# A graph layer on one core: queries' rows stored apart from the values, and the first edge pair's gathers and feature parts made in the first block

## The chip, the cores and the metric

The kernel runs on one core of one Trainium2 chip. The metric is the device time of one execution in microseconds (us). A core has five instruction streams that work side by side: TensorE (PE, matrix products), VectorE (DVE), ScalarE (ACT), GpSimd (POOL) and SyncE (SP, which here only issues DMAs). POOL and ACT issue DMAs too.

## The reference

One layer on N = 1250 nodes and E = 20000 edges with 512 features and 8 heads of 64: graph attention over the edges, a linear attention beside it, and a small quantised feed-forward behind both. Edges are sorted by destination. The part that the change touches is the graph attention:

```python
x_cat = jnp.concatenate([node_feat[src], node_feat[dst], edge_feat], axis=-1)
r = x_cat @ Wr.T + br
q = (node_feat @ Wq.T + bq).reshape(n, H, D)
k = (r @ Wk.T + bk).reshape(e, H, D)
v = (r @ Wv.T + bv).reshape(e, H, D)
a = jnp.einsum('ehd,ehd->eh', q[dst], k) * scaler
amax = jax.ops.segment_max(a, dst, num_segments=n)
ae = jnp.exp(a - amax[dst])
asum = jax.ops.segment_sum(ae, dst, num_segments=n)
attn = ae / asum[dst]
m = v * attn[..., None]
out = jax.ops.segment_sum(m, dst, num_segments=n).reshape(n, H * D)
```

## The kernel before

The program has two blocks with a barrier of all engines between them: `prologue` (the first block) and `edges_and_ending`. Every product in fp32 precision is made as three products of a high and a low part (`_hi`, `_lo`: ACT copies to the high part, DVE subtracts it for the low part).

**First block.** Weights are multiplied together first (`fold(part)`: 96 products each; part 0 for sources, 1 for destinations, 2 for edge features), so that a node's and an edge's share of keys and values is one product each. Then `source(t)` makes the rows of `kv_table` for the ten node tiles t of 128 nodes. Behind `fold(1)` comes the **destination stage**: for each t, PE makes the queries `destination_q`, the own key share `destination_k` and the own value share `destination_v`; DVE adds biases (`add_q`, `own_scores`, `add_v2`), writes the queries' rows with their own scores into `q_out` (two buffers) and the values into `v2_out` (two buffers); SP stores them to `q_table` and `v2_table` (`store_nodes(t)`). In the profile, names ending in a digit lose it: `v_out` and `v_table` are `v2_out` and `v2_table`.

Between these, PE makes `cuts(k)` for 40 quads k of four edge tiles: products of `onehot` (made by DVE in `one_hots(k)`) with `is_end16`. ACT copies each result to `cut_out` (two buffers), and POOL stores it to `cut_rows`. The chain of one quad is DVE one-hots, PE `cuts(k)`, ACT copy k, POOL store k. PE's `cuts(k)` waits for copy k - 2, and ACT's copy k waits until store k - 2 has landed. ACT also runs `sign_group` (12 row comparisons each) in between, and at k = 0, 6, 12 and 18 issues a **clear**: a DMA that fills one 2.6 MB `merge` table with its start values.

The program order on PE is, per t: `cuts(4t-2)`, `cuts(4t-1)`, k(t), `cuts(4t)`, v(t), `cuts(4t+1)`, q(t+2). On DVE, per t: `add_q(t+1)`, `own_scores(t)`, for some t a `rank_group`, `one_hots(4t+4)`, `(4t+5)`, `add_v2(t)`, `one_hots(4t+6)`, `(4t+7)`. The waits that guard the two buffers are:

```python
def add_q(t):      # and add_v2(t) alike
    if t >= 2:
        dve.wait_ge(stored[u], 16 * (NT // 2) + 32 * (t // 2))
```

`stored[u]` counts the stores of queries and of values together, so each of them waits until both stores of t - 2 have landed. `fold(2)` ends the block on PE; `evict(2)` on ACT and DVE splits its eight banks, and the barrier follows.

**Second block.** It runs over 79 pairs p of edge tiles. SP loads the pair's features (`efT`, pair 0's in `first_ef` already in the first block) and rows of indices; POOL gathers `kv` by source and `qc` by destination and `old` from the merge tables by indirect DMA, and stores `new`. PE makes `keys` (psK, 12 products a tile) and `values` (psV) of two tiles, then `sort_scores(p)`, which needs DVE's scores of the pair (`add_k`, `times_q`, `sum_scores`, `split_scores`, `rank_one_hots`). At the block's start, in the kernel before, come POOL's `fetch_kv(0)` and `fetch_q(0)` and, for pair 0, ACT's `high_part(0)` and DVE's `low_part(0)`. Behind the pairs comes the ending (linear attention, output, feed-forward).

Of the kernel before, what the change touches and what calls it, by code (L numbers as in the profile page):

```python
# [12 lines left out]
F32 = mybir.dt.float32  # L13
# [3 lines left out]
ALU = mybir.AluOpType  # L17
# [42 lines left out]
def layer(nc, x, src_col, dst_col, dst_row, ef, WqT, bq, Wr, br, WkT, bk, WvT, bv, WoT, bo, gamma, beta,  # L60
# [10 lines left out]
    with top:  # L71
# [20 lines left out]
        with ExitStack() as early:  # L92
# [12 lines left out]
            prologue(nc, ef, ef_in[0], first_ef, x, WqT, bq, Wr, br, WkT, bk, WvT, bv, src_col, dst_col, dst_row, q_table, kv_table, v2_table, merge,  # L105
# [7 lines left out]
            edges_and_ending(nc, ef, ef_in, first_ef, q_table, kv_table, merge, ident, M_hi, M_lo, dst_rows, end_rows, cut_rows,  # L113
# [5 lines left out]
def prologue(nc, ef, first_ef_in, first_ef, x, WqT, bq, Wr, br, WkT, bk, WvT, bv, src_col, dst_col, dst_row, q_table, kv_table, v2_table, merge,  # L119
# [3 lines left out]
    with ExitStack() as ctx:  # L123
# [12 lines left out]
        Wq_hi = sb("Wq_hi", [P, C, D], F32R)  # L136
        Wq_lo = sb("Wq_lo", [P, C, D], F32R)
# [11 lines left out]
        kv_out = sb("kv_out", [P, 2, 2 * D])  # L149
# [20 lines left out]
        hi_split, lo_split, br_hi_ready, br_lo_ready = sem("hi_split"), sem("lo_split"), sem("br_hi_ready"), sem("br_lo_ready")  # L170
# [5 lines left out]
        q_added, kd_added, own_step, v2_added = sem("q_added"), sem("kd_added"), sem("own_step"), sem("v2_added")  # L176
        stored = [sem(f"nodes_stored{i}") for i in range(2)]
        tables_out, cleared = sem("tables_out"), sem("cleared")
# [35 lines left out]
        def _(sp):  # L214
# [52 lines left out]
            for i in range(2):  # L267
                sp.wait_ge(stored[i], 48 * (NT // 2))

        @block.gpsimd  # L270
        def _(pool):
# [29 lines left out]
            for k, (lo, n) in enumerate(quads):  # L301
                if k == 2:
                    load_block(LATE + 2)
                if k == 6:
# [7 lines left out]
                           ends_out[0:ET - P, 1, :]).then_inc(tables_out, 16)  # L312
            pool.wait_ge(tables_out, 16 * 3)
# [1877 lines left out]
```

## Time and profile before

| | |
|---|---|
| runs of the kernel before | 1622.1 us median of 3 (1619.85 to 1623.33) |
| the profiled execution's own time | 1626.55 us |
| its span in the trace | 1624.8 us |
| PE busy | 1551.1 us, 95% of the span |
| DVE, ACT, POOL busy | 77%, 65%, 43% |
| DMA mean | 185 GB/s |

All positions in the trace are us from the span's start. An engine's row gives when it began and how long it took; in square brackets stands how long the engine had stood idle before it, and what the profile takes to have released it. Where a wait has several semaphores the profile names the one that came last, and where the engine named had long been done it was another. The granted clock of PE (PEclk) is 1.00 at 2.4 GHz and 0.50 at 1.2 GHz.

### The profile page before, as it was taken

What the parts mean: (1) busy time and instruction counts of PE and PEld (TensorE: products, weight loads), DVE (VectorE), ACT (ScalarE), POOL (GpSimd) and SP (SyncE); (2) the same over time, 40 slices, a digit from 0 to 9 for tenths busy, and PEclk for the clock granted to TensorE, in tenths of its full rate; (3) what the DMA queues carried; (4) which work ended last, traced back from release to release, by engine and by line L of the source; (5) the groups of instructions that cost most, each with busy time, mean ns of one, the idle gap of its engine ahead of it and who ended that gap; (6) DMA issues with size and microseconds to landing.
All of it is one profiled execution on the core that took longest, in us unless ns stands there. A gap on an engine that the chain in (4) does not pass through costs nothing. (4 is left out here: it accounts for less than half of the span.)

```text
span 1624.8 us, 27304 instructions
## 1 busy us (share of the span) xinstructions
PE 1551.1 (95%) x7334; PEld 1202.1 (74%) x7334; DVE 1256.3 (77%) x3141; ACT 1054.6 (65%) x3706; POOL 694.3 (43%) x722
## 2 busy tenths in 40 slices
PE   7999898999999999999999999999999999899996
PEld 6786676777777777777777777777777777777673
DVE  5866664887788778788788778878877878678878
ACT  3785122677777777777777777777777777567245
POOL 1001123556555555555555565555555565211001
PEclk9999999999999999999999999999999999999997
DMA  6575414666666666666676666666666666175001
GB/s 194 180 247 181 174 67 137 200 215 202 210 208 207 224 211 216 211 199 199 201 239 218 198 218 204 211 206 212 220 208 209 202 201 198 45 236 192 27 14 51
DMA packets 135446, 300.31 MB, mean 185 GB/s; under 512 B 34863, under 2 KB 56502, under 8 KB 135296
## 3 DMA queue, kind: packets, MB, share of 16 engines
q0 software_dynamic: 63600, 180.17, 33.6%
q1 hardware_dynamic: 66512, 107.59, 22.2%
q10 hardware_dynamic: 5184, 10.81, 1.8%
q8 instruction: 62, 1.02, 0.3%
q14 instruction: 88, 0.72, 0.1%
HBM read 271.40 MB, written 66.58 MB: 208 GB/s over the span
## 5 line engine op out<-in xcount | busy, mean ns | idle before, releaser
L1110 ACT ACTIVATE wv<-vv,expd 128x64 f32<-128x64 f32 x1248 | 314.6, 334 | 2.7
L1122 ACT ACTIVATE old<-old,expd 128x64 f32<-128x64 f32 x1232 | 302.1, 334 | 0.0
L1032 POOL DMA_INDIRECT merge<-new,put_id x157 | 162.8, 1037 | 269.2 <-DVE new L1453 236.9
L1882 PE MATMUL psK<-M_hi,efT_hi 128*128 128x512 f32 x628 | 254.3, 405 | 2.8 <-ACT efT_hi L1080 2.8
L1882 PE MATMUL psV<-M_hi,efT_hi 128*128 128x512 f32 x628 | 256.1, 408 | 0.0
L1883 PE MATMUL psK<-M_lo,efT_hi 128*128 128x512 f32 x628 | 250.0, 398 | 0.0
L1883 PE MATMUL psV<-M_lo,efT_hi 128*128 128x512 f32 x628 | 249.5, 397 | 0.0
L1003 POOL DMA_INDIRECT old<-merge,dst_id x157 | 157.8, 1005 | 142.6 <-DMA merge<-new,put_id 116.9
L1096 ACT ACTIVATE expd<-diff 128x32 f32<-128x32 f32 (+1 forms) x79 | 18.1, 229 | 289.3 <-DVE diff L1432 289.3
L1003 POOL DMA_INDIRECT kv<-kv_table,src_id x157 | 162.3, 1034 | 66.1 <-issue 47.8
L1003 POOL DMA_INDIRECT qc<-q_table,dst_id x157 | 155.0, 987 | 54.6 <-issue 46.6
L1886 PE MATMUL psK<-M_hi,efT_lo 128*128 128x512 f32 x628 | 172.3, 396 | 0.0
L1886 PE MATMUL psV<-M_hi,efT_lo 128*128 128x512 f32 x628 | 171.9, 395 | 0.0
L1882 PEld LDWEIGHTS psK<-M_hi,efT_hi 128*128 128x128 f32 x628 | 119.0, 190 | 28.2 <-ACT efT_hi L1080 3.2
L1886 PEld LDWEIGHTS psK<-M_hi,efT_lo 128*128 128x128 f32 x628 | 118.2, 188 | 28.8
L1886 PEld LDWEIGHTS psV<-M_hi,efT_lo 128*128 128x128 f32 x628 | 118.0, 188 | 28.8
L1883 PEld LDWEIGHTS psK<-M_lo,efT_hi 128*128 128x128 f32 x628 | 119.3, 190 | 25.8
L1883 PEld LDWEIGHTS psV<-M_lo,efT_hi 128*128 128x128 f32 x628 | 119.1, 190 | 25.6
L1882 PEld LDWEIGHTS psV<-M_hi,efT_hi 128*128 128x128 f32 x628 | 118.8, 189 | 25.1
L1384 DVE TENSOR_TENSOR runs_lo<-psT,runs_hi 128x16 fp32r<-128x16 f32 (+1 forms) x79 | 13.7, 174 | 144.0 <-ACT runs_hi L1087 144.0
L1344 DVE TENSOR_TENSOR kk<-psK,kv 128x512 f32<-128x512 f32 x157 | 107.0, 681 | 13.5 <-DMA kv<-kv_table,src_id 10.0
L1353 DVE TENSOR_TENSOR kq<-kk,qc 128x520 f32<-128x520 f32 x157 | 110.0, 701 | 6.6 <-DMA qc<-q_table,dst_id 1.2
(323 smaller groups left out, 3334.7 us busy)
## 6 DMA issues: line engine op xcount, KB each, us to landing
first_ef<-in_ef_turned_dram SPq DMA_DIRECT2D x39, 512.0 KB, 5.0
efT<-in_ef_turned_dram SPq DMA_DIRECT2D x39, 512.0 KB
merge<-empty ACTq DMA_DIRECT2D x4, 2640.0 KB, 10.0
rows<-merge SPq DMA_DIRECT2D x40, 256.0 KB, 3.7
row_block<-dst_rows POOLq DMA_DIRECT2D x13, 768.0 KB, 6.1
dst_line<-dst_rows SPq DMA_DIRECT2D x78, 128.0 KB, 2.7
end_line<-end_rows SPq DMA_DIRECT2D x78, 128.0 KB, 4.3
kv_table<-kv_out SPq DMA_DIRECT2D x10, 512.0 KB, 3.2
```

The costliest lines, as they stand in the source:

```text
L1003: pool.indirect_dma_start(out=out, out_offset=None, in_=table[:, :], in_offset=bass.IndirectOffsetOnAxis(ap=ids[:, t:t + 1], axis=0)).then ...
L1032: pool.indirect_dma_start(out=merge[2 * (p % 2) + u][:, :], out_offset=bass.IndirectOffsetOnAxis(ap=put_id[:, t:t + 1], axis=0), in_=new[p ...
L1096: act.activation(expd[p % 2][:, 0:n, :, :], diff[p % 2][:, 0:n, :, :], ACT.Exp, scale=SCALE).then_inc(exp_ready, 1)
L1110: act.activation(wv[:, u, h * DH:(h + 1) * DH], vv[p % 2][:, u, h * DH:(h + 1) * DH], ACT.Copy, scale=expd[p % 2][:, u, 0, h:h + 1]).then_ ...
L1122: act.activation(rows, rows, ACT.Copy, scale=expd[p % 2][:, u, 1, h:h + 1]).then_inc(old_scaled, 1)
L1344: dve.tensor_tensor(kk[:, u, :, 0:DH], psK[u][:, :].rearrange("p (h d) -> p h d", h=H), kv[p % 2][:, u, 0:D].rearrange("p (h d) -> p h d", ...
L1353: dve.tensor_tensor(kq[:, u, :, :].rearrange("p h e -> p (h e)"), kk[:, u, :, :].rearrange("p h e -> p (h e)"), qc[p % 2][:, u, :], ALU.mu ...
L1384: dve.tensor_tensor(runs_lo[:, 0:n, :], turned_s[:, 0:n, :], runs_hi[:, 0:n, :].bitcast(F32), ALU.subtract).then_inc(runs_low, 1)
L1882: pe.matmul(out[:, :], efT_hi[b][:, u, c, :], Me_hi[:, c, col:col + D], start=c == 0, stop=False)
L1883: pe.matmul(out[:, :], efT_hi[b][:, u, c, :], Me_lo[:, c, col:col + D], start=False, stop=False)
L1886: last = pe.matmul(out[:, :], efT_lo[b][:, u, c, :], Me_hi[:, c, col:col + D], start=False, stop=c == C - 1)
```

## The change

1. **Queries' rows apart.** `store_nodes(t)` issues the queries' store first, as soon as `own_scores(t)` is done, and counts it on a semaphore of its own, `q_stored`; then it waits for the values and issues their store on `stored`. `add_q(t)` waits for the queries' store of t - 2 alone, `add_v2(t)` for the values' store alone. To free semaphores, `kd_added` is folded into `own_step` (three steps a tile), and two others into `br_split`.
2. **The first gathers.** The buffers of pair 0 (`efT_hi0`, `efT_lo0`, `kv0`, `qc0`) are placed over tensors of the first block that are dead by then (`kv_out`, `Wq_hi`, `br_hi` and `br_lo`, which are moved in memory for it). POOL issues the two gathers of `kv0` and the two of `qc0` at the end of its first-block work, behind waits that all stores of the tables have landed.
3. **The first features' parts.** ACT's `high_part(0)` and DVE's `low_part(0)` stand in the first block, between the last split of `fold(2)`'s inputs and `evict(2)`.

```diff
+            kv_in = [top.enter_context(nc.semaphore(f"kv_in{i}")) for i in range(2)]
+            q_in = [top.enter_context(nc.semaphore(f"q_in{i}")) for i in range(2)]
+            hi_ready, lo_ready = (top.enter_context(nc.semaphore(n)) for n in ("efT_hi_ready", "efT_lo_ready"))
+            with ExitStack() as place:
+                def head(name, shape, dt=F32):
+                    return place.enter_context(nc.sbuf_tensor(name, shape, dt))
+
+                efT1 = head("efT1", [P, 2, C, P])
+                efT_hi1, efT_lo1, efT_hi0, efT_lo0 = (
+                    head(n, [P, 2, C, P], F32R) for n in ("efT_hi1", "efT_lo1", "efT_hi0", "efT_lo0"))
+                kv = [head(f"kv{b}", [P, 2, 2 * D]) for b in range(2)]
+                qc = [head(f"qc{b}", [P, 2, QROW]) for b in range(2)]
+            efT, efT_hi, efT_lo = [first_ef, efT1], [efT_hi0, efT_hi1], [efT_lo0, efT_lo1]
...
         raw = sb("raw", [P, SLOTS - 2, D])
+        kv_out = sb("kv_out", [P, 2, 2 * D])
+        Wq_hi = sb("Wq_hi", [P, C, D], F32R)
+        Wq_lo = sb("Wq_lo", [P, C, D], F32R)
+        br_hi = sb("br_hi", [P, C, P], F32R)
+        br_lo = sb("br_lo", [P, C, P], F32R)
+        bias = sb("bias", [P, 2, D])
         W_hi = sb("W_hi", [P, 2, C, D], F32R)
         W_lo = sb("W_lo", [P, 2, C, D], F32R)
...
-        br_hi = sb("br_hi", [P, C, P], F32R)
-        br_lo = sb("br_lo", [P, C, P], F32R)
-        bias = sb("bias", [P, 2, D])
...
-        kv_out = sb("kv_out", [P, 2, 2 * D])
...
             def store_nodes(t):
+                sp.wait_ge(own_step, 3 * t + 3)
+                sp.dma_start(q_table[t * P:(t + 1) * P, :],
+                             q_out[:, t % 2, :, :].rearrange("p h e -> p (h e)")).then_inc(q_stored[t % 2], 16)
                 sp.wait_ge(v2_added, t + 1)
                 sp.dma_start(v2_table[t * P:(t + 1) * P, :], v2_out[:, t % 2, :]).then_inc(stored[t % 2], 16)
-                sp.wait_ge(own_step, 2 * t + 2)
-                sp.dma_start(q_table[t * P:(t + 1) * P, :],
-                             q_out[:, t % 2, :, :].rearrange("p h e -> p (h e)")).then_inc(stored[t % 2], 16)
...
             for i in range(2):
-                sp.wait_ge(stored[i], 48 * (NT // 2))
+                sp.wait_ge(stored[i], 32 * (NT // 2))
+                sp.wait_ge(q_stored[i], 16 * (NT // 2))
...
                            ends_out[0:ET - P, 1, :]).then_inc(tables_out, 16)
+            pool.wait_ge(ids_in, 32)
+            pool.wait_ge(nodes_done, destination_at("v", NT - 1))
+            for i in range(2):
+                pool.wait_ge(stored[i], 32 * (NT // 2))
+                pool.wait_ge(q_stored[i], 16 * (NT // 2))
+            for u in range(2):
+                pool.indirect_dma_start(out=kv0[:, u, :], out_offset=None, in_=kv_table[:, :],
+                                        in_offset=bass.IndirectOffsetOnAxis(ap=src_id[:, u:u + 1], axis=0)).then_inc(kv0_in, 16)
+            for u in range(2):
+                pool.indirect_dma_start(out=qc0[:, u, :], out_offset=None, in_=q_table[:, :],
+                                        in_offset=bass.IndirectOffsetOnAxis(ap=dst_id[:, u:u + 1], axis=0)).then_inc(q0_in, 16)
...
                 if t >= 2:
-                    pe.wait_ge(kd_added, t - 1)
+                    pe.wait_ge(own_step, 3 * t - 5)
...
             split_wr(2 * C + 3)
+            for i in range(2):
+                act.wait_ge(stored[i], 32 * (NT // 2))
+            act.wait_ge(first_ef_in, 16)
+            act.activation(efT_hi0[:, :, :, :], first_ef[:, :, :, :], ACT.Copy).then_inc(hi_ready, 1)
             evict(2)
...
                 u = t % 2
                 dve.wait_ge(nodes_done, destination_at("q", t))
                 if t >= 2:
-                    dve.wait_ge(stored[u], 16 * (NT // 2) + 32 * (t // 2))
+                    dve.wait_ge(q_stored[u], 16 * (t // 2))
                 dve.tensor_tensor(q_out[:, u, :, 0:DH], banks[3 * u][:, :].rearrange("p (h d) -> p h d", h=H),
...
                 dve.wait_ge(nodes_done, destination_at("k", t))
                 if t >= 1:
-                    dve.wait_ge(own_step, 2 * t - 1)
-                dve.tensor_tensor(kd[:, :], banks[3 * u + 1][:, :], bias[:, 0, :], ALU.add).then_inc(kd_added, 1)
-                dve.wait_ge(kd_added, t + 1)
+                    dve.wait_ge(own_step, 3 * t - 1)
+                dve.tensor_tensor(kd[:, :], banks[3 * u + 1][:, :], bias[:, 0, :], ALU.add).then_inc(own_step, 1)
+                dve.wait_ge(own_step, 3 * t + 1)
                 dve.wait_ge(q_added, t + 1)
-                if t >= 1:
-                    dve.wait_ge(own_step, 2 * t)
                 dve.tensor_tensor(own[:, :].rearrange("p (h d) -> p h d", h=H), kd[:, :].rearrange("p (h d) -> p h d", h=H),
                                   q_out[:, u, :, 0:DH], ALU.mult).then_inc(own_step, 1)
-                dve.wait_ge(own_step, 2 * t + 1)
+                dve.wait_ge(own_step, 3 * t + 2)
                 dve.tensor_reduce(q_out[:, u, :, DH], own[:, :].rearrange("p (h d) -> p h d", h=H),
                                   AX.X, ALU.add).then_inc(own_step, 1)
...
                 if t >= 2:
-                    dve.wait_ge(stored[u], 16 * (NT // 2) + 32 * (t // 2))
+                    dve.wait_ge(stored[u], 16 * (NT // 2) + 16 * (t // 2))
                 dve.tensor_tensor(v2_out[:, u, :], banks[3 * u + 2][:, :], bias[:, 1, :], ALU.add).then_inc(v2_added, 1)
...
             split_wr(2 * C + 2)
             split_wr(2 * C + 3)
+            dve.wait_ge(hi_ready, 1)
+            dve.tensor_tensor(efT_lo0[:, :, :, :], first_ef[:, :, :, :], efT_hi0[:, :, :, :].bitcast(F32),
+                              ALU.subtract).then_inc(lo_ready, 1)
             evict(2)
...
-            efT = [first_ef, loop("efT1", [P, 2, C, P])]
-            efT_hi, efT_lo = [None, None], [None, None]
-            for b in (1, 0):
-                efT_hi[b], efT_lo[b] = (loop(f"{n}{b}", [P, 2, C, P], F32R) for n in ("efT_hi", "efT_lo"))
-            kv = loop_two("kv", [P, 2, 2 * D])
-            qc = loop_two("qc", [P, 2, QROW])
+            loop("place_of_head", [P, 5 * 2 * C * P + 2 * 2 * 2 * D + 2 * 2 * QROW])
...
-            fetch_kv(0)
-            fetch_q(0)
             for p in range(PAIRS + 2):
                 if p + 1 < PAIRS:
...
-            high_part(0)
             for p in range(PAIRS):
...
             dve.wait_ge(ones_placed, 1)
-            low_part(0)
             for p in range(PAIRS):
```

How the instructions stand, at three places. First SP, in the destination stage, before: the rows of two tiles t (`v_table`, `q_table` are the stores, in square brackets the semaphores that they wait for).

```order
35 L264 DMA first_ef<-in_ef_turned_dram 128x1024 [waits lo_split]
36 L234 DMA v_table<-v_out 128x512 [waits v2_added]
37 L236 DMA q_table<-q_out 128x520 [waits own_step]
38 L234 DMA v_table<-v_out 128x512 [waits v2_added]
39 L236 DMA q_table<-q_out 128x520 [waits own_step]
```

And SP at the same place after the change.

```order
35 L278 DMA first_ef<-in_ef_turned_dram 128x1024 [waits lo_split]
36 L248 DMA q_table<-q_out 128x520 [waits own_step]
37 L251 DMA v_table<-v_out 128x512 [waits v2_added]
38 L248 DMA q_table<-q_out 128x520 [waits own_step]
39 L251 DMA v_table<-v_out 128x512 [waits v2_added]
```

In each tile the queries' store moved ahead of the values' store.

Second POOL, at the boundary of the blocks (the two branches are the end of the first block and the start of the second), before.

```order
25 L310 DMA end_rows<-ends_out 128x128 [waits cut_copied]
26 L311 DMA end_rows<-ends_out 29x128
27 L123 UNCONDITIONAL_BRANCH [waits cut_stored0,cut_stored1,cleared,tables_out]
28 L1000 UNCONDITIONAL_BRANCH [waits barrier_Pool_Activation_PE_DVE_SP_gather]
29 L1003 DMA kv<-kv_table,src_id 128x1024 x2
30 L1003 DMA qc<-q_table,dst_id 128x520 x4
31 L1003 DMA kv<-kv_table,src_id 128x1024 x2
```

POOL at the same place after the change.

```order
25 L325 DMA end_rows<-ends_out 128x128 [waits cut_copied]
26 L326 DMA end_rows<-ends_out 29x128
27 L334 DMA kv<-kv_table,src_id 128x1024 [waits queries_stored0,nodes_stored1,nodes_stored0,queries_stored1,nodes_done,ids_in]
28 L334 DMA kv<-kv_table,src_id 128x1024
29 L337 DMA qc<-q_table,dst_id 128x520 x2
30 L136 UNCONDITIONAL_BRANCH [waits cut_stored0,cut_stored1,cleared,tables_out]
31 L1026 UNCONDITIONAL_BRANCH [waits barrier_Pool_Activation_PE_DVE_SP_gather]
32 L1029 DMA qc<-q_table,dst_id 128x520 x2
33 L1029 DMA kv<-kv_table,src_id 128x1024 x2
```

The four gathers of pair 0 moved ahead of the branch; behind it stand pair 1's.

Third ACT, at the same boundary, before.

```order
123 L461 ACTIVATE wr_hi<-raw 128x512 [waits raw_in0,rounds]
124 L461 ACTIVATE wr_hi<-raw 128x512 [waits raw_in1,rounds]
125 L476 ACTIVATE M_hi<-bank 128x512 [waits folded] x8
126 L123 UNCONDITIONAL_BRANCH
127 L1073 UNCONDITIONAL_BRANCH [waits barrier_Pool_Activation_PE_DVE_SP_release]
128 L1080 ACTIVATE efT_hi<-first_ef 128x1024 [waits ef_in0]
129 L1080 ACTIVATE efT_hi<-efT 128x1024 [waits ef_in1]
```

ACT at the same place after the change.

```order
124 L487 ACTIVATE wr_hi<-raw 128x512 [waits raw_in1,rounds]
125 L575 ACTIVATE efT_hi<-first_ef 128x1024 [waits ef_in0,nodes_stored1,nodes_stored0]
126 L502 ACTIVATE M_hi<-bank 128x512 [waits folded] x8
127 L136 UNCONDITIONAL_BRANCH
128 L1097 UNCONDITIONAL_BRANCH [waits barrier_Pool_Activation_PE_DVE_SP_release]
129 L1104 ACTIVATE efT_hi<-efT 128x1024 [waits ef_in1]
```

The high part of `first_ef` moved ahead of the eight evictions and the branch; DVE's low part moved alike.

## Rows read from the trace of the kernel before

**Rows 1.** Busy time by stretch, in the pairs: PE, PEld, DVE, ACT, POOL, PEclk, DMA share, GB/s

```profile
300.00:700.00 400.00, 394.04 (x1866) 307.87 (x1865) 324.79 (x733) 292.14 (x1071) 224.72 (x223) 1.00 0.65 209
```

**Rows 2.** Waits, 140 to 300 us: us in total, times, longest

```profile
PE bank L395 <- DVE onehot L666: 8.3, 3, 5.1
```

**Rows 3.** Timeline of PE, destination stage: start, us, line, operation

```profile
141.99 0.38 PE L395 MATMUL bank<-onehot,is_end 128*1 128x128 bf16 x4
...
145.29 0.38 PE L395 MATMUL bank<-onehot,is_end 128*1 128x128 bf16 x4
...
151.62 0.59 PE L395 MATMUL bank<-onehot,is_end 128*1 128x128 bf16 x4 [2.64 <-DVE onehot L666]
...
157.56 0.43 PE L395 MATMUL bank<-onehot,is_end 128*1 128x128 bf16 x4
...
182.95 0.59 PE L395 MATMUL bank<-onehot,is_end 128*1 128x128 bf16 x4 [5.07 <-DVE onehot L666]
...
188.69 0.38 PE L395 MATMUL bank<-onehot,is_end 128*1 128x128 bf16 x4
```

**Rows 4.** Busy time by stretch around two stops of PE, columns as Rows 1

```profile
148.00:163.00 15.00, 12.36 (x51) 8.65 (x50) 7.08 (x36) 6.11 (x23) 2.67 (x6) 0.77 0.63 220
...
260.00:268.00 8.00, 5.23 (x17) 3.83 (x16) 3.15 (x5) 2.10 (x3) 4.13 (x4) 0.79 0.50 141
```

**Rows 5.** Timeline of DVE, destination stage

```profile
176.11 0.69 DVE L674 TENSOR_TENSOR q_out<-bank,bq_all 128x512 f32<-128x512 f32 x1 [8.01 <-DMA q_table<-q_out]
```

**Rows 6.** Timeline of SP's DMA issues, destination stage

```profile
166.93 1.26 SPq L236 DMA_DIRECT2D q_table<-q_out  x1
```

**Rows 7.** DMA, 152.2 to 156 us: packets, MB, share by queue; landing us

```profile
q10 hardware_dynamic: 693, 1.46, 102.8%
...
cut_rows<-cut_out POOLq DMA_DIRECT2D x2, 2.0 KB, 6.5
```

**Rows 8.** Timeline of ACT, destination stage

```profile
145.79 0.59 ACT L539 ACTIVATE cut_out<-bank 1x512 f32<-1x512 f32 x1 [4.04 <-DMA cut_rows<-cut_out]
...
150.91 1.05 ACT L539 ACTIVATE cut_out<-bank 1x512 f32<-1x512 f32 x2
...
176.97 1.07 ACT L539 ACTIVATE cut_out<-bank 1x512 f32<-1x512 f32 x2 [4.41 <-DMA cut_rows<-cut_out]
```

**Rows 9.** DMA, 140 to 143 us

```profile
DMA packets 396, 1.02 MB, mean 340 GB/s; under 512 B 68, under 2 KB 68, under 8 KB 396
...
cut_rows<-cut_out POOLq DMA_DIRECT2D x2, 2.0 KB, 4.0
```

**Rows 10.** Timeline of POOL at the block boundary

```profile
243.99 0.54 POOL L311 DMA_DIRECT2D end_rows<-ends_out  x1
262.88 1.04 POOL L1003 DMA_INDIRECT kv<-kv_table,src_id  x1 [18.35 <-POOLq L123]
```

**Rows 11.** Timeline of PE, block boundary and pairs 0 and 1

```profile
263.26 0.62 PE L1882 MATMUL psK<-M_hi,efT_hi 128*128 128x512 f32 x1 [2.77 <-ACT efT_hi L1080]
...
273.31 0.40 PE L1882 MATMUL psV<-M_hi,efT_hi 128*128 128x512 f32 x1
...
275.18 1.10 PE L1886 MATMUL psV<-M_hi,efT_lo 128*128 128x512 f32 x4
280.43 0.23 PE L1909 MATMUL psO<-to_rank,score_hi 128*8 128x128 f32 x1 [4.15 <-DVE to_rank L1323]
...
280.74 0.73 PE L1882 MATMUL psK<-M_hi,efT_hi 128*128 128x512 f32 x1
...
284.14 1.09 PE L1886 MATMUL psK<-M_hi,efT_lo 128*128 128x512 f32 x4
```

**Rows 12.** Timeline of DVE, pair 0

```profile
274.26 0.69 DVE L1344 TENSOR_TENSOR kk<-psK,kv 128x512 f32<-128x512 f32 x1 [9.73 <-DMA kv<-kv_table,src_id]
...
279.96 0.42 DVE L1323 TENSOR_TENSOR to_rank<-iota_row,rank 128x256 fp32r<-128x256 f32 x1
```

**Rows 13.** DMA issues, 262 to 285 us

```profile
first_ef<-in_ef_turned_dram SPq DMA_DIRECT2D x1, 512.0 KB, 12.5
```

More of the change, by code:

```diff
@@ L104, in layer @@
             ef_in = [top.enter_context(nc.semaphore(f"ef_in{i}")) for i in range(2)]
[L105 removed]
+            kv_in = [top.enter_context(nc.semaphore(f"kv_in{i}")) for i in range(2)]
[10 more added lines that the diff above has]
+            efT, efT_hi, efT_lo = [first_ef, efT1], [efT_hi0, efT_hi1], [efT_lo0, efT_lo1]
+            prologue(nc, ef, ef_in[0], first_ef, efT_hi0, efT_lo0, hi_ready, lo_ready, kv[0], kv_in[0], qc[0], q_in[0], x, WqT, bq, Wr, br, WkT, bk, WvT, bv, src_col, dst_col, dst_row, q_table, kv_table, v2_table, merge,
                      dst_rows, end_rows, cut_rows, ident, xT_hi, xT_lo, M_hi, M_lo, src_id, dst_id, put_id, dst_f, rank,
@@ L112, in layer @@
             wq_lo = early.enter_context(nc.sbuf_tensor("wq_lo", [P, C, D], F32R, side="right"))
-            edges_and_ending(nc, ef, ef_in, first_ef, q_table, kv_table, merge, ident, M_hi, M_lo, dst_rows, end_rows, cut_rows,
+            edges_and_ending(nc, ef, ef_in, efT, efT_hi, efT_lo, hi_ready, lo_ready, kv, kv_in, qc, q_in, q_table, kv_table, merge, ident, M_hi, M_lo, dst_rows, end_rows, cut_rows,
                              src_id, dst_id, put_id, dst_f, rank, iota_row, iota_col, w_qkv, w_raw, wq_hi, wq_lo,
@@ L116, in layer, with prologue @@
                              res, wp, wp_lo, gT, later, out, stored)
-def prologue(nc, ef, first_ef_in, first_ef, x, WqT, bq, Wr, br, WkT, bk, WvT, bv, src_col, dst_col, dst_row, q_table, kv_table, v2_table, merge,
+def prologue(nc, ef, first_ef_in, first_ef, efT_hi0, efT_lo0, hi_ready, lo_ready, kv0, kv0_in, qc0, q0_in, x, WqT, bq, Wr, br, WkT, bk, WvT, bv, src_col, dst_col, dst_row, q_table, kv_table, v2_table, merge,
              dst_rows, end_rows, cut_rows, ident, xT_hi, xT_lo, M_hi, M_lo, src_id, dst_id, put_id, dst_f, rank,
@@ L169, in prologue @@
         bias_in, ids_in, rows_cast, consts = sem("bias_in"), sem("ids_in"), sem("rows_cast"), sem("consts")
-        hi_split, lo_split, br_hi_ready, br_lo_ready = sem("hi_split"), sem("lo_split"), sem("br_hi_ready"), sem("br_lo_ready")
+        hi_split, lo_split, br_split = sem("hi_split"), sem("lo_split"), sem("br_split")
         rounds, folded, m_hi, m_lo = sem("rounds"), sem("folded"), sem("m_hi"), sem("m_lo")
@@ L175, in prologue @@
         nodes_done, ks_copied, vs_copied = sem("nodes_done"), sem("ks_copied"), sem("vs_copied")
-        q_added, kd_added, own_step, v2_added = sem("q_added"), sem("kd_added"), sem("own_step"), sem("v2_added")
+        q_added, own_step, v2_added = sem("q_added"), sem("own_step"), sem("v2_added")
         stored = [sem(f"nodes_stored{i}") for i in range(2)]
+        q_stored = [sem(f"queries_stored{i}") for i in range(2)]
         tables_out, cleared = sem("tables_out"), sem("cleared")
@@ L403, in between_edge_part @@
                 if i == 1:
-                    pe.wait_ge(kd_added, NT)
+                    pe.wait_ge(own_step, 3 * NT - 2)
                 if i == 3:
@@ L418, in _ @@
             fold(0)
-            pe.wait_ge(br_lo_ready, 1)
+            pe.wait_ge(br_split, 2)
             for side in range(2):
@@ L497, in _ @@
                     act.wait_ge(bias_in, 16)
-                    act.activation(br_hi[:, :, :], bc(br_col[:, :], P), ACT.Copy).then_inc(br_hi_ready, 1)
+                    act.activation(br_hi[:, :, :], bc(br_col[:, :], P), ACT.Copy).then_inc(br_split, 1)
             for t in range(4):
@@ L602, in _ @@
                 if rc == 0:
-                    dve.wait_ge(br_hi_ready, 1)
+                    dve.wait_ge(br_split, 1)
                     dve.tensor_tensor(br_lo[:, :, :], bc(br_col[:, :], P), br_hi[:, :, :].bitcast(F32),
-                                      ALU.subtract).then_inc(br_lo_ready, 1)
+                                      ALU.subtract).then_inc(br_split, 1)
             for t in range(4):
@@ L774, in ending_tensors, with edges_and_ending @@
             y, yT_lo, fst, fmv, fsd, xs, hs, xn, xr, xq, xqT, hid, hq, hqT, ys, fy)
-def edges_and_ending(nc, ef, ef_in, first_ef, q_table, kv_table, merge, ident, Me_hi, Me_lo, dst_rows, end_rows, cut_rows,
+def edges_and_ending(nc, ef, ef_in, efT, efT_hi, efT_lo, hi_ready, lo_ready, kv, kv_in, qc, q_in, q_table, kv_table, merge, ident, Me_hi, Me_lo, dst_rows, end_rows, cut_rows,
                      src_id, dst_id, put_id, dst_f, rank, iota_row, iota_col, w_qkv, w_raw, wq_hi, wq_lo, xT_hi, xT_lo,
@@ L847, in edges_and_ending @@
         row_in, cut_in = ([sem(f"{n}{b}") for b in range(2)] for n in ("row_in", "cut_in"))
-        kv_in, q_in, old_in, put = ([sem(f"{n}{b}") for b in range(2)] for n in ("kv_in", "q_in", "old_in", "put"))
+        old_in, put = ([sem(f"{n}{b}") for b in range(2)] for n in ("old_in", "put"))
         def landed(p):
             return 16 * sum(tiles_of(k) for k in range(p % 2, p + 1, 2))
-        hi_ready, lo_ready, ke_done, ve_done = sem("efT_hi_ready"), sem("efT_lo_ready"), sem("k_edges"), sem("v_edges")
+        ke_done, ve_done = sem("k_edges"), sem("v_edges")
         ones_placed, onehots = sem("ones_placed"), sem("onehots")
```

2 lines of the change are left out of this document (removed).

## The prediction

> **What bounds the kernel now.** First the busy time by stretch in the pairs: PE is busy 394.04 of 400 us at full clock, the next engine, DVE, 324.79 [rows 1]. From pair 2 on PE therefore sets the pace, and whatever makes PE start there earlier moves the whole rest of the run. So I looked for PE's idle time before that, in the list of waits and then in PE's timeline from 140 to 290 us. In the destination stage PE stands 8.3 us in three waits, the longest 5.1 [rows 2]; the two large ones are 2.64 us at 151.62 and 5.07 us at 182.95 [rows 3]. At the block boundary it stands 2.77 us, and 4.15 us at 280.43 before pair 0's scores are sorted [rows 11]. The reader should see a second loss behind each: the granted clock, 0.77 in the stretch around the first and 0.79 around the boundary [rows 4], that is, a piece at 1.2 GHz between pieces at 2.4. Its price can be read: from one `cuts` to the next with a product between is 3.30 us undisturbed (141.99 to 145.29), but 5.94 us behind the first wait (151.62 to 157.56) and 5.74 behind the second (182.95 to 188.69) [rows 3]. So the clock costs 2.64 and 2.44 us on top of the idle time.
>
> **Who causes them.** The second wait: DVE stood 8.01 us until 176.11 at `add_q(4)`, for the queries' store of t = 2 [rows 5], which SP issued at 166.93 [rows 6], so 9.2 us from issue to landing. PE then waits for one-hots that stand behind it on DVE. The first wait is named DVE's too, but those one-hots (quad 7) were made long before; what `cuts(7)` also needs is ACT's copy of quad 5, and that stands in the row of two copies from 150.91 [rows 8], behind a `sign_group` which itself began after copy 4. Copy 4 was held 4.04 us, to 145.79, by the landing of the store of quad 2 [rows 8].
>
> **Why a store lands so late.** From 152.2 to 156 us, behind a clear's issue, only the ACT queue's packets ran, 693 of them at 102.8% of the engines, and cut rows issued there took 6.5 us to land [rows 7]. A store that is issued into a clear waits for it; one that is issued ahead of it doesn't. The Trainium skill (DMA: Bandwidth & Descriptors, section Queues, rings and completion order) says that each DMA engine serves the queues with work in turn, a packet at a time. The trace disagrees here: with stores of two other queues outstanding it shows a single queue's 693 packets. By that rule small stores would pass a clear, and the third case below would have no ground.
>
> **Part 1, queries' rows apart.** No instruction is added but one wait; the number of stores stays. The queries' store leaves right after `own_scores(t)`, thus ahead of the one-hots and, at some t, a rank group and the values' sum; and `add_q(t+1)` no longer waits for the values' store. Stage by stage: PE's k(2) would end near 156.8, so the store of t = 2 leaves near 159, ahead of the clear at k = 12, instead of at 166.93 behind its issue. Then it lands well before DVE wants the buffer for `add_q(4)`. DVE has no other long wait in the tile, so quad 16's one-hots are ready about 3.5 us before PE asks. The second wait goes entirely: 5.07 + 2.44 = 7.5 us. What is late next there is ACT's copy 14, which `cuts(16)` needs: it starts at 176.97 [rows 8] against PE's wish at 182.95 - 5.07 = 177.88 [rows 3], 0.3 us in time if a copy takes some 0.6.
>
> The first wait is hardly touched, since it belongs to ACT. Only one of its causes moves: the store of quad 2 landed 4.0 us after its issue, in a stretch with 1.02 MB at 340 GB/s [rows 9]. The queries' store of t = 0, 260 KB, leaves that stretch (it would be issued some 5 us earlier): 0.26 MB / 340 GB/s = 0.8 us. Copy 4, the sign group and copy 5 follow by as much. Bounds: nothing (0) if the landing doesn't depend on it, and 2.64 + 2.64 = 5.3 us if copy 5 comes in time. I take 0.8, idle time only, because 1.8 us of idle remains and every stop of that order in this trace had the low clock behind it. The third wait, the remaining 0.6 us of the 8.3, I leave. Part 1: 7.5 + 0.8 = 8.3 us.
>
> **Part 2, the first gathers.** In the kernel before, POOL is free at 243.99 + 0.54 = 244.5 and then idle for 18.35 us up to its first gather at 262.88 [rows 10]. DVE's first sum waits 9.73 us for it until 274.26, and `to_rank` of pair 0 is only done at 280.4 [rows 12]; PE ended pair 0 at 276.28 (275.18 + 1.10) and waits 4.15 us for it [rows 11]. After the change the four gathers are issued from about 244.5, at some 1.3 us each (until 250), while PE still makes `fold(2)`, whose DMA traffic is nearly nil; their landing needs at most the 12.5 us of the slowest transfer in the crowded start [rows 13], so by 262.5 in the worst case, and DVE wants them at about 266. DVE then follows PE: `to_rank` about 272.5, before PE's end of pair 0 at 275.4. The 4.15 us go. With them goes the low clock behind: the eight products from 280.74 to 284.14 took 3.40 us, the same eight at full clock 275.18 - 273.31 = 1.87 [rows 11], thus 1.53 more. Part 2: 5.7 us. Next in line is pair 1's data; the gathers and loads of pairs 1 and 2 start as before at the block's start with 1.6 MB less ahead of them.
>
> **Part 3, the first parts.** ACT's copy (1.06 us) and DVE's subtraction (1.23) go into a hole of about 5 us on both engines between the last split and the evictions; they are covered by PE's `fold(2)`. If the cover were gone they would cost their 2.3 us. PE's start in the second block no longer follows ACT's copy. Its idle time of 2.77 us [rows 11] holds the eviction and the barrier as well, which stay; I count 0.9 of the copy's 1.06 as gained, since PE must load its first weights. Bounds 0 and 1.1. I leave the low clock behind the boundary as it is: 1.9 us of idle remains. If it stayed at full clock, 1.5 us more would be gained.
>
> **The sum.** 8.3 + 5.7 + 0.9 = 14.9 us off the profiled execution's own 1626.55 (span 1624.8 and 1.75 around it) gives 1611.6. The median of the runs, 1622.1, is 4.4 below that execution; the same 14.9 off it gives **1607.2 us**. Nothing later gives it back: PE paces pairs 2 to 78 [rows 1].
>
> **The ways it could go.**
> - *As above*, 1607.2, chance 0.50; its own range 1604.5 to 1609.5 (the clock at the boundary and the unknown of each part).
> - *ACT's chain comes free too.* Copy 5 is in time, since the store of quad 2 lands as fast as an undisturbed one. For it: 2.5 us earlier would be nearly the 2.64 needed. Against it: the row block of 768 KB and the clears stay. Another 1.84 + 2.64 = 4.5 us: 1602.7. Chance 0.18.
> - *The cut chain takes the place of the queries' wait.* Copy 14 has only 0.3 us of slack and its stores run beside a clear, 6.5 us to land [rows 7]. If PE then stops 2 us at `cuts(16)` and the clock falls as before: 2.0 + 2.4 back, 1611.6. Chance 0.17.
> - *The second block starts as before*: gathers are early, but pair 1's features or gathers stop PE instead, since PE now asks 5 us sooner. Only part 1 stays: 1622.1 - 8.3 = 1613.8. Against it: less is outstanding. Chance 0.09.
> - *Slower.* One mechanism: with all requests of pairs 1 and 2 made at once, `efT` of pair 1 lands late, PE stops before pair 1 and falls to the low clock. It needs 12.5 us at worst [rows 13] from 263.4, thus 276 and a copy of 1.06, against 275.7: 1.4 us of stop. To decide it would have to land over 15 us later, 28 us after issue; at 32 us the time is 1626. Chance 0.02.
> - The rest, 0.04, lies about no change (a store or gather held by something that no row shows).
>
> A measurement of this kernel tells 0.2% (3.2 us) from no change. All cases but the last two are beyond it: faster 0.93, same 0.05, slower 0.02. The range 1601.0 to 1612.5 reaches over the first three cases, 0.85, and leaves out the tails of each.
>
> **What would show it.** In the profile after: no wait of `add_q` for a store above 1 us; PE without idle time near 178 to 183 and at full clock there; PE's wait near 151 still there, 1 to 2.6 us, and the clock low behind it; POOL's gathers of `kv` from 244 to 250 less the shift; PE's first psK product 1.7 to 2 us behind the last of `fold(2)`; no wait before `sort_scores(0)`; pairs of the same length as before. Wrong would be: a new wait at `cuts(16)` or near k = 18 released by ACT's copies or stores of cut rows; a wait of ACT for `efT` that PE follows; or the gathers of pair 0 issued only at the barrier.

## The result and the profile after

The changed kernel takes 1605.17 us (median of 5 runs, 1602.33 to 1606.27), the kernel before 1622.1 us (1619.85 to 1623.33, 5 runs). The ratio is 0.9893, with a 95% interval of 0.988 to 0.9907: 16.9 us or 1.1% faster. The forecast was 1607.2 us, 14.9 less.

The page of the changed kernel, first busy times:

```profile
span 1603.4 us, 27308 instructions
PE 1540.9 (96%) x7334; PEld 1194.8 (75%) x7334; DVE 1257.7 (78%) x3141; ACT 1054.7 (66%) x3706; POOL 688.4 (43%) x722
```

PE's own waits from 100 to 300 us, where [rows 2] had 8.3 us in the destination stage alone:

```profile
PE psK L1904 <- PEq L136: 1.7, 1, 1.7
PE bank L421 <- ACT cut_out L565: 1.1, 2, 0.8
PE bank L421 <- DVE onehot L696: 0.5, 1, 0.5
```

The first of these is the block boundary. What is left at the place of the first stop of [rows 3] stands in PE's timeline, with the product and the `cuts` behind it:

```profile
146.94 0.38 PE L421 MATMUL bank<-onehot,is_end 128*1 128x128 bf16 x4 [0.82 <-ACT cut_out L565]
...
150.21 0.38 PE L421 MATMUL bank<-onehot,is_end 128*1 128x128 bf16 x4
```

From one `cuts` to the next it is now 3.27 us behind the stop, where [rows 3] show 5.94: the clock didn't fall. Over 45 us of the stage it shows as this (windows; busy us and count of PE, PEld, DVE, ACT, POOL, then granted clock, DMA share, GB/s), first before, then after:

```profile
145.00:190.00 45.00, 37.29 (x166) 26.59 (x165) 27.13 (x114) 12.80 (x40) 6.99 (x15) 0.85 0.44 158
```

```profile
145.00:190.00 45.00, 43.91 (x228) 31.73 (x227) 34.14 (x132) 12.43 (x29) 9.92 (x20) 1.00 0.64 237
```

The two windows don't hold quite the same work, but both of the first profile's stops lie in its window. PE's idle time in these 45 us falls from 7.7 to 1.1 us, and the granted clock rises from 0.85 to 1.00: both losses that the prediction read there are gone.

**What each store does now.** SP's and ACT's issues in the stage, and DVE's `add_q(4)` and `add_q(5)`:

```profile
141.39 0.32 SPq L248 DMA_DIRECT2D q_table<-q_out  x1
...
145.66 0.37 ACTq L558 DMA_DIRECT2D merge<-empty  x1
...
152.48 0.32 SPq L248 DMA_DIRECT2D q_table<-q_out  x1
...
159.17 0.69 DVE L704 TENSOR_TENSOR q_out<-bank,bq_all 128x512 f32<-128x512 f32 x1
...
159.20 0.37 ACTq L558 DMA_DIRECT2D merge<-empty  x1
...
162.93 0.32 SPq L248 DMA_DIRECT2D q_table<-q_out  x1
...
170.53 0.69 DVE L704 TENSOR_TENSOR q_out<-bank,bq_all 128x512 f32<-128x512 f32 x1 [0.62 <-DMA q_table<-q_out]
```

The queries' store of t = 2 leaves at 152.48, 6.7 us ahead of the clear at 159.20, and lands in 3.9 us; in [rows 6] it left at 166.93, behind a clear, and took 9.2. `add_q(4)` runs at 159.17 without a wait, against 176.11 in [rows 5]. The next store, t = 3 at 162.93, does fall behind a clear and takes 7.5 us, but DVE comes for its buffer so late that it waits 0.62 us. The landing times come from the DMA view of 152 to 155 us and of 160 to 164:

```profile
q_table<-q_out SPq DMA_DIRECT2D x1, 260.0 KB, 3.9
```

```profile
q_table<-q_out SPq DMA_DIRECT2D x1, 260.0 KB, 7.5
```

DVE's waits for stores of queries fell from 27.0 us in six waits to 0.6 in one.

**The start of the second block.** POOL, then PE:

```profile
230.24 1.04 POOL L334 DMA_INDIRECT kv<-kv_table,src_id  x1 [0.30 <-issue]
...
234.13 0.96 POOL L337 DMA_INDIRECT qc<-q_table,dst_id  x1 [0.30 <-issue]
248.18 0.95 POOL L1029 DMA_INDIRECT qc<-q_table,dst_id  x1 [13.09 <-POOLq L136]
```

```profile
247.58 0.47 PE L1904 MATMUL psK<-M_hi,efT_hi 128*128 128x512 f32 x1 [1.69 <-PEq L136]
258.87 0.22 PE L1931 MATMUL psO<-to_rank,score_hi 128*8 128x128 f32 x1
```

All four gathers are issued before PE is through with the block, the hole before `psK` is 1.69 us instead of 2.77, and the 4.15 us before `sort_scores(0)` of [rows 11] are gone.

**A ledger by stage.** Read from PE's rows: S1 is the time from the last product of `fold(1)` to the first of `fold(2)` (the destination stage), S2 from the last of `fold(2)` to `sort_scores(2)`. `fold(2)` itself is 22.5 us in every profile. From pair 2 on, executions differ by more than the change is worth with nothing changed (the changed kernel took 1041.8 us from `sort_scores(2)` to `sort_scores(75)` in one profile and 1061.5 in another), so parts of the change are compared in these stretches, and whole runs only where they were timed in turn with the kernel before.

| profile | S1 | S2 |
|---|---|---|
| kernel before; the same again | 114.5; 112.7 | 48.4; 47.8 |
| changed kernel; the same again | 102.7; 102.8 | 39.9; 39.9 |
| stores apart only | 103.5 | 48.3 |
| gathers and parts only; the same again | 111.6; 114.4 | 39.9; 39.9 |
| change, gathers back | 103.1 | 47.8 |
| change, parts back | 102.6 | 41.0 |
| change, values' store first | 112.9 | 39.9 |
| change, both waits | 108.5 | 39.9 |
| before, clears late | 109.2 | 49.9 |
| before, signs earlier | 105.7 | 48.5 |
| change, signs earlier | 105.4 | 39.9 |

The change takes 9.9 to 11.8 us out of S1 and 7.9 to 8.5 out of S2, 17.8 to 20.3 together, by which pair of profiles one takes. The two spans first profiled differ by 21.4 us; 2.8 of that lie ahead of S1, where nothing of the change works: both have two stops of about one us near 40 us, and only in the profile before 3.4 us of half clock follow. (One other profile of the fourteen, experiment 2's second, has the same.) The rest of the spans tells the other way: from `sort_scores(2)` to the end the kernel before took 1316.7 and 1315.2 us, the changed kernel 1318.4 and 1338.1. So in the first pair of profiles 1.7 us of the 20.3 don't reach the end. Whether the change causes that or it is the spread of executions is not shown.

### The profile page after: what moved, and what is told of

It reads as the page before. It is cut to its first block and busy times, and to the rows that moved or that the text cites. A ratio compares the mean times of both kernels' runs of the same rounds, so it can differ in the third digit from the quotient of the medians.

```text
span 1603.4 us, 27308 instructions
## 1 busy us (share of the span) xinstructions
PE 1540.9 (96%) x7334; PEld 1194.8 (75%) x7334; DVE 1257.7 (78%) x3141; ACT 1054.7 (66%) x3706; POOL 688.4 (43%) x722
## 5 line engine op out<-in xcount | busy, mean ns | idle before, releaser
L1029 POOL DMA_INDIRECT kv<-kv_table,src_id x155 | 155.3, 1002 | 47.8 <-issue 47.5
L1385 DVE TENSOR_REDUCE score<-kq 128x8 f32<-128x520 f32 x157 | 109.1, 695 | 5.4
```

The source lines that it names most:

```text
L1029: pool.indirect_dma_start(out=out, out_offset=None, in_=table[:, :], in_offset=bass.IndirectOffsetOnAxis(ap=ids[:, t:t + 1], axis=0)).then ...
L1385: dve.tensor_reduce(score[p % 2][:, u, :], kq[:, u, :, :], AX.X, ALU.add).then_inc(score_step, 1)
```

## The experiments

The kernels of the first four experiments (of the second, its first run) ran beside the kernel before, which there took from 1623.2 to 1649.5 us in 34 of its 35 runs and 1679.8 in one. So of them only the ratio and the stretches are used, and all whole-run differences between them are within their intervals.

**1. The stores apart, alone.** The changed kernel with gathers and parts at the start of the second block again:

```diff
-            for u in range(2):
-                pool.indirect_dma_start(out=kv0[:, u, :], out_offset=None, in_=kv_table[:, :],
...
-            act.activation(efT_hi0[:, :, :, :], first_ef[:, :, :, :], ACT.Copy).then_inc(hi_ready, 1)
...
+            fetch_kv(0)
+            fetch_q(0)
...
+            high_part(0)
...
+            low_part(0)
```

> Part 1 alone: queries' stores apart and first, but the first gathers and the first high and low parts back in the second block. Theory A (the ledger of the profile after): PE's two stops in the destination stage go, 1.8 and 5.1 us of idle, and the low clock behind both, 2.6 and 2.4, together 11.9 us: 1610. The gap of 2.8 us at the boundary and the 4.2 us before pair 0's scores are sorted stay, with the low clock behind both. Rival B (as my prediction priced it, ACT's chain hardly touched): 8.3 us, 1613.8. Rival C (the surplus over the forecast comes from the run's start, not from part 1): the stop near 147 us is 1.8 us or more here.

Measured: 1621.47 us, ratio 0.9928 (0.9891 to 0.9964). S1 is 103.5 and S2 48.3: the whole gain of the destination stage and nothing of the boundary's. The first stop was 0.88 us, and S1 is 9.2 to 11.0 us shorter. So theory A holds: the surplus over the forecast is the stage's own (B had 8.3 us in all) and doesn't come from the run's start (C). PE's timeline has both holes of before back:

```profile
248.38 0.51 PE L1890 MATMUL psK<-M_hi,efT_hi 128*128 128x512 f32 x1 [2.77 <-ACT efT_hi L1088]
265.39 0.23 PE L1917 MATMUL psO<-to_rank,score_hi 128*8 128x128 f32 x1 [3.99 <-DVE to_rank L1331]
```

**2. Gathers and parts, alone.** The values' store goes first again, and each sum waits for both stores of t - 2:

```diff
+                sp.wait_ge(v2_added, t + 1)
+                sp.dma_start(v2_table[t * P:(t + 1) * P, :], v2_out[:, t % 2, :]).then_inc(stored[t % 2], 16)
                 sp.wait_ge(own_step, 3 * t + 3)
...
-                sp.wait_ge(v2_added, t + 1)
-                sp.dma_start(v2_table[t * P:(t + 1) * P, :], v2_out[:, t % 2, :]).then_inc(stored[t % 2], 16)
...
                     dve.wait_ge(q_stored[u], 16 * (t // 2))
+                    dve.wait_ge(stored[u], 16 * (NT // 2) + 16 * (t // 2))
...
                     dve.wait_ge(stored[u], 16 * (NT // 2) + 16 * (t // 2))
+                    dve.wait_ge(q_stored[u], 16 * (t // 2))
```

> Parts 2 and 3 alone: values stored first again, and both sums wait again for both stores of t - 2. Theory A: the destination stage shows the two stops of before again (2.6 and 5.1 us, low clock behind both), the boundary looks as after the change: 4.2 + 1.5 for the gathers, 1.1 for the parts, and 1.7 if the clock stays full at the boundary, 6.8 to 8.5 us: 1614 to 1615.3. Rival: if the parts don't add up (one hides the other), this and the run before it together give back clearly more or less than the 16.9 us of the whole.

Measured: 0.9945 (0.9912 to 0.9979). S2 is 39.9, and the second stop is back, 6.64 us:

```profile
177.08 0.58 PE L421 MATMUL bank<-onehot,is_end 128*1 128x128 bf16 x4 [6.64 <-DVE onehot L696]
```

But the first stop was only 0.68 us, with the stores in their old order. That didn't fit the view that the queries' early store shortens it, so the kernel was run once more.

> Parts 2 and 3 alone, once more. In the first run of it PE's first stop was 0.7 us only, although the queries' store of t = 0 was issued as late as before the change. If it is the position of that store that delays the landing of quad 2's store, 2 us or more of stop should be seen in this second look; if the landing is 2 us again, something else in this kernel (addresses, counting apart) does it.

It had 2.22 us there, 6.54 at the second, and 1617.97 us in the one run. So the landing that decides the first stop differs from one execution to the next. ACT's wait before copy 4 was 3.5 to 4.2 us in five profiles with the old order and 2.08 in the first run of these parts; it was 1.5 to 2.3 in all six with the early store and the sign groups in their place.

**3. The gathers back, alone** (`fetch_kv(0)` and `fetch_q(0)` at the second block's start; parts stay early).

> The changed kernel with only the four gathers of pair 0 back at the start of the second block. Theory: DVE's first sum waits for them some 9 us again, PE stands 4 us before the sorting of pair 0 and has the low clock behind it: 5.7 us over the changed kernel, 1610.9. Rival: the parts made early let PE start sooner, so PE waits longer for the same gathers and part 3's gain is lost as well: 5.7 + 1.1, 1612.

Measured: 0.9935 (0.9901 to 0.997), S2 47.8, as much as before. PE's start is early (1.69 us of idle), but it pays that back at the scores:

```profile
266.27 0.28 PE L1922 MATMUL psO<-to_rank,score_hi 128*8 128x128 f32 x1 [6.20 <-DVE to_rank L1337]
```

The gathers' path ends last here, so what PE gains at the boundary lengthens its wait for them, 4.15 to 6.20 us. Early parts are worth nothing without early gathers. In S2 that is 7.9 us over the changed kernel; the theory had 5.7, the rival that loses part 3's gain as well had 6.8 and was right in kind.

**4. The parts back, alone** (`high_part(0)` and `low_part(0)` at the second block's start; gathers stay early).

> The changed kernel with only the high and low part of pair 0 back in the second block. Theory: PE's gap at the boundary is 2.8 instead of 1.7 us, 1.1 us more, and the granted clock falls to 0.5 behind it as before the change, another 1.5 to 1.7: 1607.9. Rival: the clock's fall there is not tied to the gap's length and comes and goes from run to run: 1606.3, and a profile that may show full clock behind 2.8 us of idle.

Measured: 0.9928 (0.9895 to 0.9961), S2 41.0. So early parts are worth 1.1 us beside early gathers, which is the hole's 2.77 less 1.69:

```profile
247.80 0.51 PE L1899 MATMUL psK<-M_hi,efT_hi 128*128 128x512 f32 x1 [2.77 <-ACT efT_hi L1097]
```

The clock stayed at 2.4 GHz behind this hole, as in no other profile with a hole of 2.77 (five had 3.4 to 6.8 us at 1.2 GHz behind it). So the expectation's rival is what this profile shows, and 1.1 us is the price at full clock; where the clock falls it would be more.

**5. The change again**, timed beside the next three.

> The changed kernel once more, on the chip of the three runs beside it, so that they can be compared, and for the low clock behind gaps of 1 to 1.7 us in a second profile: ratio 0.989 to 0.990. If the clock's falls at 41 us and at the block boundary come and go from run to run, this profile may show one of them.

Measured: 1613.91 us where the kernel before had 1625.64, ratio 0.9917 (0.9891 to 0.9942). The clock fell neither at 41 us nor at the boundary.

**6. Is it the order of the stores, or the waits apart?** The changed kernel with the values' store first, the waits still apart (the first half of experiment 2's edit).

> The changed kernel with the values' store ahead of the queries' again, each still counted apart. It tells early issue from split waits. Theory: it is the early issue that counts. The queries' store of t = 0 then stands in the stretch of the row block again, quad 2's store lands 4 us after its issue, PE stops 2.6 us near 147 with the low clock behind it, and the queries' stores of t = 1 and t = 2 lie in the clears again, so that DVE waits for them some 6 to 8 us and PE stops near 178: 1614 to 1617, most of part 1 lost. Rival: the split of the waits counts, and the time stays at 1605 to 1608.

Measured: 0.9953 (0.9927 to 0.9979). S1 is 112.9: nothing of the stage's gain is left. PE's timeline:

```profile
148.39 0.38 PE L421 MATMUL bank<-onehot,is_end 128*1 128x128 bf16 x4 [2.13 <-DVE onehot L696]
...
179.79 0.59 PE L421 MATMUL bank<-onehot,is_end 128*1 128x128 bf16 x4 [6.30 <-DVE onehot L696]
```

and DVE's waits from 140 to 230 us:

```profile
DVE q_out L704 <- DMA q_table<-q_out: 26.8, 7, 7.9
```

**7. The queries' store first, but each sum waits for both stores** (the second half of that edit).

> The changed kernel with the queries' store first, but each sum waiting for both stores of t - 2 again. Theory: add_q(3) then waits for the values' store of t = 1, issued at 147 behind the clear and landing near 155, and add_q(5) for that of t = 3, issued at 168 in the second clear and landing near 174; PE has some 3 us of slack behind DVE there, so it stops less than before the change: 0 to 3 us of idle in all, 1605 to 1610. Rival: the values' store takes the whole place of the queries' store, PE stops 5 us near 178 and the clock falls: 1612.

Measured: 0.9951 (0.9926 to 0.9976), S1 108.5, about half of the gain. The theory's 0 to 3 us of idle time was wrong and the rival right, the values' store takes the queries' place:

```profile
DVE q_out L705 <- DMA v_table<-v_out: 20.3, 6, 6.4
```

```profile
174.26 0.38 PE L421 MATMUL bank<-onehot,is_end 128*1 128x128 bf16 x4 [4.97 <-DVE onehot L696]
```

The first stop is gone in it (no idle time at `cuts(7)`), the second isn't, and the clock falls behind it. Both halves of part 1 are needed: the wait apart is worth nothing as long as the queries' store goes last, and the early store gives only the first stop while the sums wait for the values' too.

**8. The kernel before with the clears of k = 6, 12 and 18 made late**, to see whether the clears make the stores land late:

```diff
-                if k % 6 == 0 and k // 6 < TABLES:
-                    act.dma_start(merge[k // 6].rearrange("(t p) w -> p t w", p=P),
+                if k in (0, 22, 26, 30):
+                    act.dma_start(merge[(0, 22, 26, 30).index(k)].rearrange("(t p) w -> p t w", p=P),
```

> The kernel before with nothing changed but the time of the clears: those of the second to fourth merge table go out at quads 22, 26 and 30 instead of 6, 12 and 18. Theory (a store issued into a clear waits for it): in the destination stage DVE no longer waits 8 us for the queries' stores of t = 1 and t = 2, PE's 5.1 us near 183 go with the low clock behind them (7.5 us), the stop near 151 stays since copy 4 waits for a store ahead of the clear. Waits like these may come back near quads 22 to 34, where PE has the same slack as near quad 18, where before there was no stop: 1614.6. Rival: the stores are slow for another reason (their own size, the row blocks), and the time stays at 1622.

Measured: 0.9997 (0.9968 to 1.0027), no gain in time where 7.5 us were expected. In the stage the mechanism is plain, though. From `cuts(9)` to `cuts(16)` PE took 17.0 us (16.9 in the changed kernel), against 22.1 in the kernel before: with no clear there, the second stop is gone although the stores keep their old order and wait. The waits went where the clears went: of the six below, three stand ahead of 176 us with 3.4 us at most, the other three (5.8, 4.9 and 4.2 us) from 199 us on, and PE has a new stop of 2.49 us at 218. S1 stays 3.5 to 5.3 us shorter and S2 is 1.5 to 2.1 longer; that the remaining 1.4 to 3.8 us don't show in whole runs is within their interval.

```profile
DVE q_out L674 <- DMA q_table<-q_out: 22.8, 6, 5.8
```

**9. The first stop.** The profile before names DVE for it, the prediction named ACT's copy 5, which stands behind a sign group. The group is moved one copy ahead, in the kernel before and in the changed one:

```diff
-                if k in (0, 2, 5, 9):
-                    sign_group(LATE + (0, 2, 5, 9).index(k))
+                if k in (0, 2, 4, 9):
+                    sign_group(LATE + (0, 2, 4, 9).index(k))
```

> The kernel before with ACT's third group of 12 sign comparisons moved from quad 5 to quad 4, into ACT's wait for the landing of quad 2's store. Theory: PE's first stop belongs to ACT's copy 5, held by copy 4 plus the group behind it; with the group inside copy 4's wait, copy 5 is in time, the stop of 2.6 us near 151 and the low clock behind it (2.6) go, while the 5.1 us near 183 stay as they are: from the end of the second fold to the start of the third 114.5 - 5.3 = 109.2 us. Rival: the stop is DVE's, as the profile's release says, and stays.

> The same move of the sign group in the changed kernel, as the version that may beat both: the stop of 0.3 to 0.8 us near 147 goes, and that of 0.3 us behind it may stay, since copy 7 waits for a store inside the clear. Destination stage 102.7 - 0.8 = 101.9 us, total 1 us under the changed kernel at most, less than a measurement tells.

In the kernel before (one run, 1613.66 us, where the unchanged kernel took 1622.2 to 1627.6) the stop at `cuts(7)` was gone, so it was the copy and not the one-hots. A new one came one quad on, at `cuts(8)`:

```profile
153.18 0.38 PE L395 MATMUL bank<-onehot,is_end 128*1 128x128 bf16 x4 [2.79 <-ACT cut_out L539]
```

That the second stop stays, as was expected, was wrong: it went, with the stores still late (20.4 us of waits for them, the longest 4.7), and S1 was 105.7. The clears go out earlier there (at 145.10 and 162.00, before 150.35 and 164.82), which may be enough for that; it was not tried apart. This move of one group alone takes 7.0 to 8.8 us out of S1, against 9.9 to 11.8 for the change. In the changed kernel the same edit took away the rest of the first stop and made the same new one, 2.44 us at 151.32, behind two copies that wait for cut rows stored into a clear which is now issued earlier:

```profile
150.59 1.09 ACT L565 ACTIVATE cut_out<-bank 1x512 f32<-1x512 f32 x2 [5.87 <-DMA cut_rows<-cut_out]
```

S1 is 2.7 us longer there (105.4), where 0.8 us less was expected. Whole runs don't show it: 1607.73 us, ratio 0.9887 (0.9868 to 0.9906), against 0.9893 for the change on another occasion, intervals over each other. No version better than the changed kernel came out of it.

**10. The kernel before again**, one run, as a second set of its stretches.

> The kernel before once more, for a second look at its stops. Theory: both stops of PE come again, 2 to 3 us near 150 and 5 to 6 us near 181, each with the low clock behind it, and 2.8 and 4 us around the start of the pairs. If the first stop is small here although nothing is changed, its size is luck of the store's landing and not owed to the change.

It took 1620.33 us, with stops of 2.40 and 5.61 us in the stage; its stretches stand in the table.

## Why the prediction was right, step by step

The measured time lies 2.0 us below the likeliest case, in its own range. The mechanisms named came in, but the number is closer than the terms: in the stretches the change took 2.9 to 5.4 us more than the forecast, and whole runs show only 2.0 of it. That part of the agreement is luck.

- **The second stop, 7.5 us: right.** 5.07 us of idle and the low clock behind are gone, and for the reason given: the store of t = 2 left ahead of the clear. Experiments 2 and 6 bring the stop back, and experiment 8 shows that without a clear in that place the old order does no harm.
- **The first stop, 0.8 us: right in its cause, too small in its size.** It is ACT's (experiment 9). Copy 4 waits 1.8 us less, 2.22 for the 4.04 of [rows 8]:

```profile
141.10 0.59 ACT L565 ACTIVATE cut_out<-bank 1x512 f32<-1x512 f32 x1 [2.22 <-DMA cut_rows<-cut_out]
```

PE's stop shrank as much, from 2.64 to 0.82; I had reckoned 0.8 from bytes by throughput. The forecast also left the clock low behind what remained, and at 0.82 us it stayed full, 2.7 us more (5.94 less 3.27). This is the mis-sized term: 4.5 for 0.8 in this pair of profiles, less the 0.3 us of a new small stop at `cuts(9)`. With the 7.5 that makes 11.7, and S1 is 11.8 shorter. It isn't safe in every execution, as experiment 2's 0.68 us with late stores shows; why that landing was fast was not found. My second case, ACT's chain free, thus came in for the larger part.
- **The cut chain at `cuts(16)`, with 0.3 us of slack: held.** No profile with both halves of part 1 had a stop there.
- **Gathers, 5.7 us: right.** 4.15 us of idle and 1.5 of clock are gone. They were issued from 230.24, against 244.5 less the shift of 14.6 which PE had by then. Experiment 3 prices them at 7.9 us of S2, since the early parts alone gain nothing.
- **Parts, 0.9 us: 1.1 measured** (experiment 4). Left low in the forecast, the clock behind the boundary stayed full: [rows 11] have 17.2 us from `psK` to the scores, 4.15 of them idle, and the changed kernel takes 11.3; 17.2 less 4.15 less 11.3 is 1.7 us, near the 1.5 named as the upside.
- **The second block starts as before, or the kernel is slower:** neither came. In the eight profiles with early gathers PE had no stop between `psK` of pair 0 and `sort_scores(2)`, and S2 was 39.9 in seven of them and 41.0 in the one with the parts back.

The terms as measured make 17.8 to 20.3 us, the sum of the forecast was 14.9, and whole runs gave 16.9. Between these nothing can be shown; it is less than what the pairs vary. The forecast's sentence that nothing later gives the gain back isn't shown either: from pair 2 on the first two profiles differ by 1.7 us against the change. Part 1 and parts 2 with 3 add up: 11.0 us of S1 and 0.1 of S2 in experiment 1, 8.5 of S2 in experiment 2, 20.3 for all (against the first profile before; that experiment 2 also has 2.9 of S1 is its first run's quick landing, 0.1 in the second run). Ratios of the parts alone, 0.9928 and 0.9945, make 0.9873 if multiplied, with intervals too wide to say more.

## What to carry to other kernels

A buffer's wait is as long as the landing of the store that frees it, and that depends on what is issued ahead: make small stores leave before the large fill, and count them apart, so that no sum waits for a store that it doesn't need. Either half alone gave none or half of the gain here. When a wait is removed, ask what arrives last next: early parts were worth 1.1 us with early gathers (one profile, at full clock) and nothing without. And moving a large fill or a block of work in time moves the waits with it (experiments 8 and 9).

## What the runs showed of the hardware

- A clear holds back the stores issued behind it, for its first five to seven us and not to its end. In the changed kernel one is issued at 145.66. From 149 to 150 us only its own queue (q10) moves data; from 151 to 152 the queue of SP's stores (q1) has nearly half:

```profile
q10 hardware_dynamic: 176, 0.37, 101.7%
...
q10 hardware_dynamic: 99, 0.21, 56.4%
q1 hardware_dynamic: 82, 0.17, 46.2%
```

The values' store issued at 146.84, behind this clear, landed at 153.2, ahead of the clear (155.8). Behind the clear of 159.20, which landed at 170.3, the store issued at 162.93 landed at 170.4. A store of 256 to 260 KB took 2.0 us undisturbed (issued at 141.39, four us ahead of a clear), 2.5 to 3.9 in a clear's tail (168.37 and 152.48) and 6.4 to 9.2 when issued 1.2 to 3.7 us behind one. The view of 148 to 152 us in the changed kernel:

```profile
q10 hardware_dynamic: 644, 1.36, 91.4%
q1 hardware_dynamic: 83, 0.17, 11.7%
q0 software_dynamic: 5, 0.00, 0.1%
```

The Trainium skill (DMA: Bandwidth & Descriptors, section Queues, rings and completion order) has the engines serve their queues in turn, and a whole packet of several descriptors is drained before the next queue's. The prediction says that the trace disagrees, which goes further than the rows do: the profile's packets are some 2 KB each (1.36 MB in 644), and whether the page's packet is one of these or many isn't known here. If it is one, the rows disagree, since of 732 packets 644 are the clear's; if it is many, first one queue alone and then shares is what the rule would give. What they show in either case is that a 2 KB cut row issued there took 6.5 us. What decides which queue gets the engines was not tried.

- The clock isn't a function of the last hole's length alone. Behind the boundary's 1.69 us it stayed at 2.4 GHz in all eight profiles; behind 2.77 us it fell in five and stayed in one (experiment 4); behind two holes of one us near 40 us it fell in two profiles of fourteen.
- With its operands made ahead, PE still stands 1.69 us at the boundary between the blocks; no profile here was below it.
